# Causal masks taken out of the matrix products and put on VectorE, in an attention and expert layer on Trainium2

## The reference, cut to what matters

```
x: 8 x 1024 x 256, 16 heads of 64, latent width 64, 32 experts
q = x Wq;  latent = x Wkv_down;  k = latent Wk_up;  v = latent Wv_up
attn = q k^T / 8;  masked where key > query;  softmax over the keys
x = layernorm(x + (attn v) Wout)
top-1 router, capacity 1.25 T / E, per expert silu(x Wg) * (x Wu) Wd, times the gate
x = layernorm(x + expert output)
```

## Time and profile before

| | |
|---|---|
| median of 3 runs | 2971.61 us (2959.61 to 2977.6) |
| the profiled execution | 2956.08 us |
| its span, first to last instruction | 2954.3 us |
| mean granted TensorE clock | 0.954 of full |
| busy: PE, DVE, ACT, POOL | 2750.7, 1555.7, 1010.4, 1522.2 us |
| instructions | 38198 |

### The profile page before, as it was taken

One profiled execution on the slowest core, in us unless ns is written; L12 is line 12 of the kernel. 1 busy time (PEld: TensorE's weight loads), 2 busy tenths in 40 slices (PEclk: granted clock), 3 DMA queues, 4 the chain that ended last, 5 costly groups with the idle time before them and its releaser, 6 DMA issues.

```text
span 2954.3 us, 38198 instructions
## 1 busy us (share of the span) xinstructions
PE 2750.7 (93%) x14120; PEld 1710.8 (58%) x14120; DVE 1555.7 (53%) x3346; ACT 1010.4 (34%) x1496; POOL 1522.2 (52%) x1162
## 2 busy tenths in 40 slices
PE   7999999999999999999999999999999999959996
PEld 5555565556555565566555655566555655546664
DVE  3555546554655456554655465545655465325553
ACT  2333424342434334432334234423343243212222
POOL 0555545653565446654565356545664465513444
PEclk8899999999999999999999999999999999969998
DMA  8000001100010002000100011000100010034551
GB/s 213 15 19 16 18 8 41 32 16 11 26 47 16 12 11 62 15 15 8 56 17 15 11 29 44 16 11 16 58 15 15 10 42 19 8 118 130 158 157 64
DMA packets 97576, 119.05 MB, mean 40 GB/s; under 512 B 12992, under 2 KB 76488, under 8 KB 97392
## 3 DMA queue, kind: packets, MB, share of 16 engines
q1 hardware_dynamic: 90224, 99.98, 12.6%
q0 software_dynamic: 7168, 16.64, 1.5%
HBM read 46.91 MB, written 37.90 MB: 29 GB/s over the span
## 4 chain that ended last, share of the span: by engine, by line
PE 85%; DVE 9%; issue 2%; ACT 2%; POOL 1%; DMA 1%; SPq 0%; POOLq 0%; ACTq 0%; DVEq 0%
PE value_ps L663 19%; PE turned_ps L639 10%; PE row_ps L612 10%; PE turned_ps L645 9%; PE misc_ps L680 8%; PE misc_ps L559 7%; PE turned_ps L768 5%; PE misc_ps L672 4%; PE row_ps L615 2%; PE turned_ps L641 2%; DVE unit_max L994 2%; PE value_ps L781 2%; PE misc_ps L781 2%; DVE q_hl L980 2%; DVE q_hl L979 1%
## 5 line engine op out<-in xcount | busy, mean ns | idle before, releaser
L421 POOL TENSOR_TENSOR sums<-sums,probs 128x1024 f32<-128x1024 f32 (+3 forms) x512 | 827.7, 1617 | 543.8 <-ACT probs L846 520.6
L846 ACT ACTIVATE probs<-turned_ps 128x1024 f32<-128x1024 f32 (+3 forms) x768 | 622.6, 811 | 1228.2 <-PE turned_ps L645 1198.6
L994 DVE TENSOR_REDUCE unit_max<-row_ps 128x1 f32<-128x512 f32 (+3 forms) x1024 | 554.8, 581 | 273.1 <-PE row_ps L612 264.3
L663 PE MATMUL value_ps<-probs,lat_keys 128*64 128x512 f32 (+3 forms) x3072 | 622.2, 529 | 1.2 <-ACT probs L846 1.2
L645 PE MATMUL turned_ps<-q_max,lat_lo 65*128 65x512 f32 (+3 forms) x1536 | 613.2, 400 | 2.3 <-DMA q_max<-max_rows 2.3
L639 PE MATMUL turned_ps<-q_hl,lat_hi 128*128 128x512 f32 (+3 forms) x1536 | 597.3, 389 | 0.0
L612 PE MATMUL row_ps<-lat_hi,q_hl 128*128 128x512 f32 (+3 forms) x1536 | 469.1, 376 | 60.4 <-DVE unit_max L994 57.4
L639 PEld LDWEIGHTS turned_ps<-q_hl,lat_hi 128*128 128x128 f32 x1536 | 297.8, 194 | 200.0 <-issue 167.0
L417 POOL TENSOR_TENSOR sums<-probs 128x768 f32<-128x768 f32 (+1 forms) x128 | 268.8, 2100 | 200.6 <-ACT probs L846 200.3
L612 PEld LDWEIGHTS row_ps<-lat_hi,q_hl 128*128 128x128 f32 x1536 | 290.9, 197 | 114.4 <-DVE unit_max L994 82.8
L663 PEld LDWEIGHTS value_ps<-probs,lat_keys 128*64 128x64 f32 x3072 | 195.7, 143 | 213.1 <-issue 168.1
(11 more groups left out here) (169 smaller groups left out, 2645.8 us busy)
## 6 DMA issues: line engine op xcount, KB each, us to landing
q_max<-q_hl SPq DMA_DIRECT2D x256, 128.0 KB
slots_x<-headsT SPq DMA_DIRECT2D x40, 258.0 KB, 9.8
ex_x<-slots_x SPq DMA_DIRECT2D x64, 129.0 KB, 3.4
x_in<-in_L_attn_x_bld SPq DMA_DIRECT2D x8, 1024.0 KB
layer_out<-x_in SPq DMA_DIRECT2D x8, 1024.0 KB, 4.4
ex_w<-in_L_ffn_w_gate SPq DMA_DIRECT2D x32, 256.0 KB, 2.8
ex_w<-in_L_ffn_w_up SPq DMA_DIRECT2D x32, 256.0 KB, 3.0
ex_w<-in_L_ffn_w_down SPq DMA_DIRECT2D x32, 256.0 KB, 3.5
```

The lines of the kernel that those rows point to most:

```text
L421: nc.gpsimd.tensor_tensor(sums[c][:, :, q0:BANK], sums[c][:, :, q0:BANK], now[:, :, q0:BANK], ALU.add).then_inc(added, 1)
L663: mm = nc.tensor.matmul(value_ps[h * LD:(h + 1) * LD, q0:BANK], lat_keys[b % 2][:, j, :], probs[:, n % NPROBS, h, q0:BANK], start=(j == 0) ...
L846: nc.scalar.activation(probs[:, n % NPROBS, :, q0:BANK], turned_ps[n % 2][:, :, q0:BANK], ACT.Exp).then_inc(exp_done, 1)
L994: ins = nc.vector.tensor_reduce(dst, row_ps[n % 2][:, 0:width], AX.X, ALU.max, negate=True)
```

## The change

The two mask products are gone. For the row maximum, a float32 tile `future` of 512 columns, zero but for -1e30 above the diagonal in its last 128, is added by the instruction that takes the maximum: for units that end on the diagonal `tensor_reduce` becomes `tensor_tensor_reduce`, which adds the last `width` columns of `future` to the unit, scales by -1, takes the minimum, and writes the masked row to a bf16 tile that nobody reads. For the turned scores nothing is added: the exponential is taken of the unmasked scores, and `keep_past` then takes the minimum of the 128 x 128 diagonal blocks of both heads with a tile `keep`, which is 0 where the key is later than the query and 1e30 elsewhere. VectorE does that for the slot before at the start of each slot, ahead of EARLY and of the maxima. Both readers of the probabilities, `values` and `add_probs`, wait for it (`kept`) in diagonal slots. The order of the row score units of the later queries changes from head, key block to key block, head.

```diff
--- before.py
+++ after.py
@@ -51,10 +51,12 @@
     on_diagonal = lambda t: SLOT[t][1] >= HPB * SLOT[t][0]
 
     UNITS = ([(h, i, 0) for i in range(HPB) for h in range(2)]
-             + [(h, i, k) for i in range(HPB, NT) for h in range(2) for k in range(2)])
+             + [(h, i, k) for i in range(HPB, NT) for k in range(2) for h in range(2)])
     NU = len(UNITS)
     UNITS_AT = [range(2 * t, 2 * t + 2) for t in range(NSLOT)]
     assert NU == 2 * NSLOT
+
+    kept_by = lambda n: n // NSLOT * NT + sum(on_diagonal(t) for t in range(n % NSLOT + 1))
     NPROBS = 6
     NHEADS = NPAIR + 1
 
@@ -87,8 +89,9 @@
 
         attn = ExitStack()
         ident_bf = sb("ident_bf", [P, P], BF16, attn)
-        future_bf = sb("future_bf", [P, P], BF16, attn)
-        past_bf = sb("past_bf", [P, P], BF16, attn)
+        future = sb("future", [P, BANK], F32, attn)
+        masked_row = [sb(f"masked_row{i}", [P, BANK], BF16, attn) for i in range(2)]
+        keep = sb("keep", [P, P], F32, attn)
         before_bf = sb("before_bf", [P, P], BF16, attn)
         ones_bf = sb("ones_bf", [P, P], BF16, attn)
         ones_f = sb("ones_f", [P, LD], F32, attn)
@@ -186,7 +189,7 @@
         values_done = sem("values_done")
         value_free = sem("value_free")
         added = sem("added")
-        sums_turned = sem("sums_turned")
+        kept = sem("kept")
         inverse_done = sem("inverse_done")
         inverse_rows = sem("inverse_rows")
         normalised = sem("normalised")
@@ -370,8 +373,8 @@
             nc.gpsimd.iota(token_i[:, :], [[P, NT]], base=0, channel_multiplier=1).then_inc(const_ready, 1)
             nc.gpsimd.memset(earlier[:, :, :], 0.0).then_inc(const_ready, 1)
             nc.gpsimd.memset(ident[:, :], 0.0).then_inc(const_ready, 1)
-            nc.gpsimd.memset(future_bf[:, :], 0.0).then_inc(const_ready, 1)
-            nc.gpsimd.memset(past_bf[:, :], 0.0).then_inc(const_ready, 1)
+            nc.gpsimd.memset(future[:, :], 0.0).then_inc(const_ready, 1)
+            nc.gpsimd.memset(keep[:, :], -MASKED).then_inc(const_ready, 1)
             nc.gpsimd.memset(before_bf[:, :], 1.0).then_inc(const_ready, 1)
             nc.gpsimd.memset(ones_bf[:, :], 1.0).then_inc(const_ready, 1)
             nc.gpsimd.memset(minus_half[:, :], -0.5).then_inc(const_ready, 1)
@@ -380,10 +383,11 @@
 
             nc.gpsimd.affine_select(out=ident[:, :], in_=ident[:, :], pattern=[[-1, P]], compare_op=ALU.not_equal,
                                     fill=1.0, base=0, channel_multiplier=1).then_inc(const_ready, 1)
-            nc.gpsimd.affine_select(out=future_bf[:, :], in_=future_bf[:, :], pattern=[[-1, P]], compare_op=ALU.is_ge,
-                                    fill=MASKED, base=0, channel_multiplier=1).then_inc(const_ready, 1)
-            nc.gpsimd.affine_select(out=past_bf[:, :], in_=past_bf[:, :], pattern=[[1, P]], compare_op=ALU.is_ge,
-                                    fill=MASKED, base=0, channel_multiplier=-1).then_inc(const_ready, 1)
+            nc.gpsimd.affine_select(out=future[:, BANK - P:], in_=future[:, BANK - P:], pattern=[[-1, P]],
+                                    compare_op=ALU.is_ge, fill=MASKED, base=0, channel_multiplier=1
+                                    ).then_inc(const_ready, 1)
+            nc.gpsimd.affine_select(out=keep[:, :], in_=keep[:, :], pattern=[[1, P]], compare_op=ALU.is_ge,
+                                    fill=0.0, base=0, channel_multiplier=-1).then_inc(const_ready, 1)
             nc.gpsimd.affine_select(out=before_bf[:, :], in_=before_bf[:, :], pattern=[[1, P]], compare_op=ALU.is_gt,
                                     fill=0.0, base=0, channel_multiplier=-1).then_inc(const_ready, 1)
             nc.gpsimd.tensor_copy(expert_m[:, :], expert_i[:, :]).then_inc(const_ready, 1)
@@ -406,6 +410,8 @@
                 now = probs[:, n % NPROBS]
                 q0 = first_query(t)
                 pool.wait_ge(exp_done, n + 1)
+                if on_diagonal(t):
+                    pool.wait_ge(kept, kept_by(n))
                 if c == 0 and j == 0:
                     if gp:
                         pool.wait_ge(misc_full, MISC["sums", gp - 1, 0] + 1)
@@ -608,12 +614,8 @@
                     pe.wait_ge(max_done, n - 1)
                 k0, k1 = k * BANK, min((i + 1) * P, (k + 1) * BANK)
                 dst = row_ps[n % 2]
-                last = k1 == (i + 1) * P
-                mm = nc.tensor.matmul(dst[:, 0:k1 - k0], q_hl[gp % 2][:, h, i * P:(i + 1) * P], lat_hi[b % 2][:, k0:k1],
-                                      start=True, stop=not last)
-                if last:
-                    mm = nc.tensor.matmul(dst[:, k1 - k0 - P:k1 - k0], ident_bf[:, :], future_bf[:, :], start=False, stop=True)
-                mm.then_inc(rows_full, 1)
+                nc.tensor.matmul(dst[:, 0:k1 - k0], q_hl[gp % 2][:, h, i * P:(i + 1) * P], lat_hi[b % 2][:, k0:k1],
+                                 start=True, stop=True).then_inc(rows_full, 1)
 
             def turn_max(gp, c):
                 use = ("maxT", gp, c)
@@ -637,9 +639,6 @@
                 for h in range(2):
                     dst = turned_ps[n % 2][:, h, q0:BANK]
                     nc.tensor.matmul(dst, lat_hi[b % 2][:, keys], q_hl[gp % 2][:, h, cols], start=True, stop=False)
-                    if on_diagonal(t):
-                        nc.tensor.matmul(turned_ps[n % 2][:, h, q0:q0 + P], ident_bf[:, :], past_bf[:, :],
-                                         start=False, stop=False)
                     if h == 0 and j == 0:
                         pe.wait_ge(q_max_loaded[c], 48 * (gp + 1))
                     mm = nc.tensor.matmul(dst, lat_lo[b % 2][:, keys], q_max[:, c, h, q0:BANK], start=False, stop=True)
@@ -658,6 +657,8 @@
                             wait_emptied(pe, ("keys", b))
                     if n == n0:
                         pe.wait_ge(exp_done, n0 + 2)
+                    if on_diagonal(t):
+                        pe.wait_ge(kept, kept_by(n))
                     q0 = first_query(t)
                     for h in range(2):
                         mm = nc.tensor.matmul(value_ps[h * LD:(h + 1) * LD, q0:BANK], lat_keys[b % 2][:, j, :],
@@ -991,11 +992,25 @@
                     dve.wait_ge(misc_full, MISC["maxT", gp - 1, c] + 1)
                 dst = neg_max[0][:, at:at + 1] if c == 0 else unit_max[:, at, k:k + 1]
                 dve.wait_ge(rows_full, n + 1)
-                ins = nc.vector.tensor_reduce(dst, row_ps[n % 2][:, 0:width], AX.X, ALU.max, negate=True)
-                ins.then_inc(max_done, 1)
+                if k * BANK + width == (i + 1) * P:
+                    nc.vector.tensor_tensor_reduce(masked_row[n % 2][:, 0:width], row_ps[n % 2][:, 0:width], future[:, BANK - width:],
+                                                   scale=-1.0, scalar=-MASKED, op0=ALU.add, op1=ALU.min, accum_out=dst
+                                                   ).then_inc(max_done, 1)
+                else:
+                    nc.vector.tensor_reduce(dst, row_ps[n % 2][:, 0:width], AX.X, ALU.max, negate=True
+                                            ).then_inc(max_done, 1)
                 if u == NU - 1:
                     dve.wait_ge(max_done, n + 1)
                     nc.vector.tensor_reduce(neg_max[1][:, :], unit_max[:, :, :], AX.X, ALU.min).then_inc(max_combined, 1)
+
+            def keep_past(gp, t):
+
+                n = gp * NSLOT + t
+                if on_diagonal(t):
+                    now = probs[:, n % NPROBS, :, first_query(t):first_query(t) + P]
+                    dve.wait_ge(exp_done, n + 1)
+                    nc.vector.tensor_tensor(now, now, keep[:, :].unsqueeze(1).to_broadcast([P, 2, P]), ALU.min
+                                            ).then_inc(kept, 1)
 
             def copy_max(gp, c):
                 use = ("maxT", gp, c)
@@ -1120,6 +1135,8 @@
             for gp in range(PAIRS):
                 b, p = divmod(gp, NPAIR)
                 for t in range(NSLOT):
+                    if gp + t:
+                        keep_past(*divmod(gp * NSLOT + t - 1, NSLOT))
                     for use in EARLY.get((gp, t), []):
                         STAGES[use[0]](*use[1:])
                     if gp + 1 < PAIRS:
@@ -1132,6 +1149,7 @@
                         variance(b - 1, p)
                     if b and (p, t) in ((0, 10), (1, 2)):
                         normalise(b - 1, p)
+            keep_past(PAIRS - 1, NSLOT - 1)
             for use in ENDING:
                 if use[0] in STAGES:
                     STAGES[use[0]](*use[1:])
```

## The result

The change makes the kernel slower by 1.2%: 3007.5 us, the median of four runs (3001.3 to 3012.2), against 2972.5 for four of the kernel before. The ratio is 1.012, with an interval of 1.0087 to 1.0152. The forecast was 3013 us. The profiled execution took 3006.9 us where that of before took 2956.1: 50.8 us more, for which the prediction's sum was 41.

A forecast was written before the change was run, and what follows sets the result against it. TensorE sets the time, with VectorE close behind in some slots. Plain pairs +47, long pairs -17, start +1 and clock +10 sum to +41 us: 2997 for an execution like the profiled one, 3013 median; range 2880 to 3100.

The forecast's parts named there:

- What leaves TensorE: Mask products dropped from both score types: 3.15 us of a head pair, 200 us over 64 pairs without added waits.
- the chain's 118: Lower bound on TensorE's relief: both mask products' shares of the last-ending chain, about 59 us each, 118 us.
- The masked maximum: On VectorE, 16 of 24 row maxima per pair become two-input instructions, each 0.08 us dearer, from 0 to 0.25.
- third rival: Masked maximum costs 0.25 us more instead of 0.08, so minima miss gaps between GpSimd additions; 3093 us, chance 0.15.
- The minimum: Eight per pair on VectorE: 0.42 us free, held while a GpSimd addition of up to 2.37 us runs.
- second rival: GpSimd does not hold the minima, so some slots lose only queue places; 2950 us, chance 0.15.
- Places in the queue: Each minimum stands behind VectorE's late work of its slot, delaying TensorE; pair ends 0.85 us later, 0.95 with dearer maxima.
- TensorE works 3.15 us less and waits 4.1 us more: Balance for one plain head pair, leaving it 0.95 us longer.
- 14 long pairs, together -17: Pairs with projections or router work on TensorE gain: -1.6 us for seven, -0.8 for seven, since VectorE has time there.
- The clock: Longer slot 10 waits bring a fifth more lower-clock stretches, some ten, for +10 us; price 1.6 us each.
- The new order of the row units changes nothing in the counts: Wide row units share one slot, narrow ones the next; costed at nothing beyond the slot layout.
- TensorE keeps most of what it is relieved of: First rival: only slot 1's wait is real, a pair loses 1.55 us; 2873 us, chance 0.22.

The follow-up runs named there:

- e3: Changed kernel with no causal mask at all: no mask products, no minima or waits for them, plain row maxima; 2849.9 us, ratio to before 0.9586.
- e10: Kernel before with the new order of the row units alone; 2925.3 us, ratio to before 0.9841.
- e5: Changed kernel with an unread one-input reduction in place of each minimum, same place in the queue; 2977.6 us, ratio to before 1.0065.
- e6: Changed kernel with the row units in the order of before; 3024.1 us, ratio to before 1.0228.
- e4: Changed kernel with each minimum moved into its own slot, behind its maxima and ahead of VectorE's late work; 2857.3 us, ratio to before 0.9612.
- e8: e4 with the last q subtractions of a slot moved to the next slot, behind its maxima; 2815.8 us, ratio to before 0.952.
- e9: Changed kernel with GpSimd zeroing the diagonal blocks instead of VectorE's minima, and q subtractions one slot later; 2765.7 us, ratio to before 0.9312.

## Why the prediction came out as it did

**What leaves TensorE: right in slots without a wait, too large in all.** By the prediction's prices the masks of slots 0, 1 and 2 (two turned and two row masks each) are 0.33, 0.44 and 0.42 us. With no masks (e3) these slots are shorter by 0.32, 0.49 and 0.44. But of 3.15 us only 1.64 reach the length of the pair, since slot 10 gives back nothing to speak of (0.08) and slot 3 is longer. In all it is 109 us between the profiled executions (2956.1 to 2846.9), below even the chain's 118. And e3 has the new order of units. Against e10, in the same order, the masks give 0.99 us of the pair (34.46 to 33.47) and 79 us in all: slot 10, which gave back nothing against before, takes back 0.95 us. So the price of a mask is right where TensorE does not wait, and the 200 us for all of them were far too much.

**The masked maximum: over-estimated, with no effect.** The prediction took 0.08 us more than a reduction; it measured 0.02 at most. Two plain ones of 512 columns took 1.27 us together (574.48) where one takes 0.68, so a step is 0.59, against 0.61 for the masked ones. The third rival's mechanism exists and its price doesn't. (Its sum has a slip besides: 1.3, 0.3 and 0.2 are 1.8 us a pair and not 1.6.) The Trainium skill (VectorE: DVE Perf Modes, section Two Vector instructions with no wait between them) says that such an instruction is two; the trace agrees, with 512 reads of 82 ns under each destination, and adds that the next instruction starts together with the read.

**The minimum: 0.42 us free, held beside GpSimd: right.** Free ones took 0.42 and 0.43, held ones up to 2.09, and the mean was 791 ns. Held ones end 0.3 us after GpSimd's instructions, and a one-input reduction in the same places takes 407. The Trainium skill's rule of an exclusive lock (SBUF — State Buffer, section Who interferes with whom) is borne out for two inputs in SBUF. But its weight in the sum was wrong. The second rival put a kernel without the hold at 2950, 63 us below the forecast; e5 is 0.55% below the change, 16 us, with the lower clock of e5 in it.

**Places in the queue: right in kind, and the cause.** Slot by slot, with the table's means (clock effects included):

| | forecast, us later | measured |
|---|---|---|
| slots 1 to 4 | +1.06 | 0.92 |
| slots 5 to 8 | -0.45 | -0.42 |
| slots 9 and 10 | +0.55 | +0.39 |
| slots 11 and 0 | -0.3 | +0.16 |
| pair, with the maxima | +0.95 | +1.05 |

The waits of slot 2, where the lower clock never falls, are the queue's alone. The other rows hold some of the clock: the forecast of 0.95 was laid out at full clock, while in the 41 plain pairs the time at the lower clock grew from 154 to 231 us, which is up to 0.94 of the 1.05. That the two numbers for the pair agree is in part luck.

The wait of slot 2 was forecast at 1.6 us and is 1.31 in the pair shown. The one of slot 4 was forecast at 1; slot 4 is 0.51 longer on average and in the pair shown it has none, so one of the prediction's signs of being right, a wait of about 1 us in slot 4, did not appear. The wait of slot 10, "over 2 us", is 2.22.

"TensorE works 3.15 us less and waits 4.1 us more": both are too large. Outside its products TensorE stands 367.5 us (3005.1 less 2637.6) where it stood 203.6, so 164 more, 2.6 a pair. Its busy time fell by 113 us; with up to 36 added by the clock (below) that is a relief of 149 us at most, 2.3 a pair. The two errors, 1.5 and at least 0.8 us, cancel in part.

**The sum.** By pairs, with the trace's means: 41 plain ones at +1.05 are +43; eight pairs that load the next batch go from 36.56 to 37.87, +10; the seven first pairs of a batch from 64.27 to 63.24, -7; the seven second ones from 39.98 to 40.40, +3. Together +49 of 50.8. Against the terms of the prediction:
- 50 x 0.95 = 47 and +10 for the clock: 57 forecast, 53 measured for the 49 pairs, clock included.
- "14 long pairs, together -17": they gave -4, the first pairs -7 for -11 and the second ones +3 for -6. In the second pairs the prediction took a gain where there is none.
- The clock: the mechanism is there, its size was too small. Time at the lower clock grew by 72 us (167 to 239), 11 stretches more. At 1.2 GHz, half the full clock, a product takes up to twice as long (the prediction has 3.2 us for 1.6), so this is up to 36 us of the 50.8, inside the pairs' numbers, against +10 put down. Of the terms of the sum this may be the one that was mis-sized most. The count was good (ten more stretches forecast, 11 measured), but ten at its own price of 1.6 us are 16 and not 10, and the mean stretch grew too, from 4.1 to 4.6 us. "Slots 11 and 0" is one place where it shows.
- "The new order of the row units changes nothing in the counts": the counts stayed, and the time did not. The order gives 1.1% in the change and 1.6% in the kernel before. The masks' own part is thus about +2.3% by e6, and the forecast, which took none of the order's gain, came close in part by luck: it under-estimated the clock's price and over-estimated the gain of the long pairs, and these errors and the order's gain have opposite signs.

**The rivals.** "TensorE keeps most of what it is relieved of" fell to the queue places, as argued: with those moved (e4) the kernel takes 2857 us, near the 2873 worked out for this rival. But some 1.6% of e4's 3.9% is the order's, which the rival did not count; 2.3%, some 68 us, is left of its 99 and of the 200 us of relief. So with `keep_past` a few lines further down the change would have been the gain that this rival forecast, though TensorE does not keep most of what it is relieved of even then.

## What to carry to other kernels

Work that is moved from the bound engine to one that idles 47% of the time can cost far more by its place in that engine's queue than by its busy time: here 512 minima cost about 0.3% behind the maxima of their own slot and 5% more behind the late work of it. The place is not all: in the tighter schedule of e8, taking them off VectorE altogether gave another 2.1% (e9). Before moving work, find the instruction that now ends last ahead of it in the queue and the one behind it that someone waits for; and look at the waits that exist already, for what the bound engine is relieved of disappears there (slot 10 here, whose repair alone brought 3.2% without any change to the masks). An order of units that keeps all counts is not free to change: it gave 1.1 to 1.6%, where the masks' own part cost 2.3%. So put it into both kernels before you compare them.

## What the runs showed of the hardware that was not expected

- VectorE's accumulating maximum writes 128 x 512 bf16 and a maximum for 0.61 us a step, where the plain reduction has 0.60; its separate accumulator read (82 ns) overlaps the start of the next instruction.
- The hold seems to go both ways, though no run isolates it. GpSimd's division of 128 x 512 has a mean of 1.28 us in the kernel before and in e9, where VectorE has no minima, and of 1.35 in the changed kernel (line 435; 1.45 at 574.23 above, where it starts before the held minimum has ended). In e4, with the minima in other places, it is 1.28 again.
- The granted clock moved more than the waits did. Exchanging the two middle ones of every four of the later row units, four exchanges a pair, shortened the wait for the maxima by 9 us and the time at 1.2 GHz by 68 us (e10).
- GpSimd's select in place over 128 x 256 float32 takes 412 ns, as long as VectorE's free minimum of the same size (0.42).
